# Attention with rotary embedding on one core: one q/k projection per turn with halves exchanged by DMA, and maxima turned by 128 stationary columns

## Chip, cores and metric

One Trainium2 chip, one core. The metric is the device time of one execution in microseconds (us), the median of several runs.

## The reference, cut to what matters

The whole program is a four-part network over a 2048x128 input. The change touches its first part alone, an attention layer with 16 heads of 64:

```
qkv = x @ qkv_w + qkv_b                 # x 2048x128, per head q, k, v of 2048x64
q, k = rope(q), rope(k)                 # r0 = t0*cos - t1*sin ; r1 = t1*cos + t0*sin
attn = softmax(q @ k.T / 8)             # 2048x2048 per head
out  = (attn @ v) @ out_w + out_b
x    = layernorm(x + out)
```

The other three parts (a local attention with a gated layer, a recurrent mixer, a gated layer) are left as they are.

## The kernel before, in words

`mha_heads` (from L137) computes the attention. Float32 accuracy is made of two float16 parts of each operand, so a product is three matmuls (high by high, low by high, high by low), all into float32 PSUM. The even and the odd features of a head are laid out as two halves of 32 partitions, q in partitions 0 to 63 and k in 64 to 127.

**Turns and steps.** The main loop runs over 512 steps p. A turn e is one head and one chunk of 512 queries (64 turns), and has 8 steps j; a step handles 256 keys. While turn e is attended to, the projections of turn g = e + 6 are made; they exist for the first 58 turns, e = 0 to 57. Every engine has its own list of work, written out by hand in program order, and waits only on semaphores.

**TensorE, one step (L402 to L435).** `scores(p)`: four matmuls of 512 columns into one of two PSUM buffers `p_s`. `maxima(p+12)`: two matmuls of 512 columns, one into each bank of `p_m`; each waits until VectorE has reduced what that bank held before (L341). `weigh(p-3)`: 24 matmuls of 64 or 65 columns that add up the output in `p_o`; in the turn's fourth step (j = 3) a new output begins, and its first half waits for `o_free`, that VectorE has divided and taken out the old one (L366). Beside that, in a turn: at j = 0 `project` (three matmuls of 512 columns, L302 to L304) with the weights whose halves are exchanged ("turned", L423), at j = 1 `project` with the plain ones into the same bank `p_a` once the first was read (L425, L426), at j = 5 `turn_max` (L347: the 4 columns of negated maxima are the stationary operand, a 128x128 identity moves), at j = 6 the projection of v (12 short matmuls).

**ScalarE, one step.** Two exponentials of 128x1024 (L484, L487), once in float16, once in float32. **GpSimd, one step.** One subtraction of 128x1024 (L278) that makes the low part; in one turn of four it also splits the next head's weights, 320 columns, into two parts (L239, L241).

**VectorE, in order, for a turn (L595 to L622).** Two maxima reductions per step (L542). At j = 0, between them, `rotate_sin` (L499: rot = (p_a + bias) * sin); at j = 1 `rotate_cos` (L505, in place in p_a); at j = 2, after the step's first reduction, `rotate_sum` (L511: p_a += rot), then `normalise` of the turn before (L563, L565; it posts `o_free`), then the step's second reduction. At j = 3 `negate_max` (L549) and `high` (L516), at j = 4 `low` (L522), at j = 5 `max_rows` (L555), at j = 7 the two parts of v.

**SyncE.** It issues all DMAs from one queue (L218 to L231). For each g: at a head's first chunk, the next head's weights into `w_head` (L223); after `hi_done` four copies of 64 KB from `hi` to q and k tiles (L225 to L228); after `lo_done` two more (L230, L231). None of them is needed within the turn.

Of the kernel before, what the change touches and what calls it, by code (L numbers as in the profile page):

```python
# [6 lines left out]
ALU = mybir.AluOpType  # L7
# [104 lines left out]
BY_DVE = 4  # L112
LEAD_M = 12
W_COLS = 5 * HD
W_TURNED, W_QK, W_V = slice(2 * HD, 4 * HD), slice(0, 2 * HD), slice(4 * HD, 5 * HD)

EXP_SHIFT = 12 * float(np.log(2.0)) * HD ** 0.5

# [18 lines left out]
def mha_heads(nc, x_sb, ident, a, attn, wo):  # L137

    IC = HEADS * HD // P
    with Scope(nc, "ah_") as sc:  # L140
# [12 lines left out]
        vh = sc.sb("v_hi", [P, SETS, KT, VW], F16)  # L153
        vl = sc.sb("v_lo", [P, SETS, KT, HD], F16)
        rot = sc.sb("rot_sin", [P, CH])
        hi = sc.sb("hi", [P, 2, CH], F16)
        lo = sc.sb("lo", [P, 2, CH], F16)
        part = sc.sb("part_max", [P, TPC, 4])
        negm = sc.sb("neg_max", [P, TPC], F16)
        identh = sc.sb("ident_f16", [P, P], F16)  # L160
        pb = sc.sb("probs", [P, RP, 2, CH])
        ph = sc.sb("probs_hi", [P, RW, 2, CH], F16)
# [10 lines left out]
        (ident_in, w_in, bias_in, x_turned, xh_ready, xl_ready, v_ones, zeroed, consts, w_hi_done,  # L173
         w_split, turned_ready, proj_ready, rot_done, cos_done, r_done, hi_done, lo_done, v_ready, vh_done,
         vl_done, m_ready, maxed, m_done, m_turned, mrow_ready, s_ready, exp_done, lo_pool, o_ready, rcp_done,
         o_free, wo_in, bias_turned, bias_done, biased, evac_t, evac_p) = (sc.sem(n) for n in (
             "ident_in", "w_in", "bias_in", "x_turned", "xh_ready", "xl_ready", "v_ones", "zeroed", "consts",
             "w_hi_done", "w_split", "turned_ready", "proj_ready", "rot_done", "cos_done", "r_done",
             "hi_done", "lo_done", "v_ready", "vh_done", "vl_done", "m_ready", "maxed", "m_done", "m_turned",
             "mrow_ready", "s_ready", "exp_done", "lo_pool", "o_ready", "rcp_done", "o_free", "wo_in",  # L180
             "bias_turned", "bias_done", "biased", "evac_t", "evac_p"))
        x_in = [sc.sem(f"x_in{c}") for c in range(NCH)]
        table_in = [sc.sem(f"table_in{c}") for c in range(NCH)]
        spread = [sc.sem(f"spread{b}") for b in range(2)]
        SPREAD = 6 * 16
        LAST_G = TURNS - 1

        def turned_bank(g):
# [11 lines left out]
        with nc.Block() as block:  # L200

            @block.sync
            def _(sp):
                sp.dma_start(ident[:, :], a["ident"]).then_inc(ident_in, 16)
                for c in range(NCH):
                    sp.dma_start(x_sb[:, c * TPC:(c + 1) * TPC, :],
                                 a["x"][c * CH:(c + 1) * CH, :].rearrange("(t p) d -> p t d", p=P)).then_inc(x_in[c], 16)
                    if c == 0:
                        sp.dma_start(w32[:, :], a["w_heads"][0]).then_inc(w_in, 16)
                        sp.dma_start(bqk[:, :, :], a["b_qk"]).then_inc(bias_in, 16)  # L210
                    sp.dma_start(sin[:, chunk(c)], a["sin"][:, chunk(c)]).then_inc(table_in[c], 16)
                    sp.dma_start(cos[:, chunk(c)], a["cos"][:, chunk(c)]).then_inc(table_in[c], 16)
                sp.wait_ge(w_split, 1)
                sp.dma_start(w32[:, :], a["w_heads"][1]).then_inc(w_in, 16)
                sp.dma_start(bo[:, :, :], a["b_o"]).then_inc(wo_in, 16)
                sp.dma_start(bv[:, :], a["b_v"]).then_inc(wo_in, 16)
                sp.dma_start(wo[:, :, :], a["wo_a"].rearrange("(c p) d -> p c d", p=P)).then_inc(wo_in, 16)
                for g in range(TURNS):  # L218
                    h, c = divmod(g, QC)
                    to, cs = h % SETS, chunk(c)  # L220
                    if c == 0 and 1 <= h < LAST:
                        sp.wait_ge(w_split, h + 1)
                        sp.dma_start(w32[:, :], a["w_heads"][h + 1]).then_inc(w_in, 16)  # L223
                    sp.wait_ge(hi_done, g + 1)
                    sp.dma_start(ka[0:HD, to, cs], hi[HD:P, g % 2, :]).then_inc(spread[g % 2], 16)  # L225
                    sp.dma_start(kb[HD:P, to, cs], hi[HD:P, g % 2, :]).then_inc(spread[g % 2], 16)
                    sp.dma_start(qa[0:HD, to, cs], hi[0:HD, g % 2, :]).then_inc(spread[g % 2], 16)
                    sp.dma_start(qa[HD:P, to, cs], hi[0:HD, g % 2, :]).then_inc(spread[g % 2], 16)  # L228
                    sp.wait_ge(lo_done, g + 1)
                    sp.dma_start(ka[HD:P, to, cs], lo[HD:P, g % 2, :]).then_inc(spread[g % 2], 16)  # L230
                    sp.dma_start(qb[HD:P, to, cs], lo[0:HD, g % 2, :]).then_inc(spread[g % 2], 16)  # L231

            @block.gpsimd
            def _(pool):
                def split_weights(h):
                    pool.wait_ge(w_in, 16 * (h + 1))
                    if h >= 2:
                        pool.wait_ge(v_ready, QC * (h - 1))
                    pool.tensor_copy(wh[:, h % 2, :], w32[:, :]).then_inc(w_hi_done, 1)  # L239
                    pool.wait_ge(w_hi_done, h + 1)  # L240
                    pool.tensor_tensor(wl[:, h % 2, :], w32[:, :], wh[:, h % 2, :], ALU.subtract).then_inc(w_split, 1)  # L241

                split_weights(0)
                pool.memset(vh[:, :, :, HD:VW], 1.0).then_inc(v_ones, 1)
# [39 lines left out]
            def _(pe):  # L284
# [59 lines left out]

                def turn_max(e):
                    pe.wait_ge(m_done, e + 1)
                    pe.matmul(p_a[0:TPC, 0:P], negm[:, :], identh[:, :], start=True, stop=True).then_inc(m_turned, 1)  # L347

                def scores(p):
                    e, j = divmod(p, PAIRS_A)  # L350
# [51 lines left out]
                for p in range(STEPS_A):  # L402
                    e, j = divmod(p, PAIRS_A)
                    g = e + LEAD_G
                    if j == 0:
                        pe.wait_ge(mrow_ready, e + 1)
                    last = j == LAG - 1 and p >= LAG
                    if not last:
                        scores(p)
                    if last:  # L410
                        weigh(p - LAG, 0)
                    if p + LEAD_M < STEPS_A:
                        maxima(p + LEAD_M, (0,))
                    if last:
                        weigh(p - LAG, 1)
                        scores(p)
                    elif p >= LAG:
                        weigh(p - LAG, 0)
                    if p + LEAD_M < STEPS_A:
                        maxima(p + LEAD_M, (1,))  # L420
                    if j == 0 and g <= LAST_G:
                        pe.wait_ge(vl_done, g)
                        project(turned_bank(g), g, W_TURNED, turned_ready)  # L423
                    if j == 1 and g <= LAST_G:
                        pe.wait_ge(rot_done, g + 1)  # L425
                        project(proj_bank(g), g, W_QK, proj_ready)  # L426
                    if j == 5 and e + 1 < TURNS:
                        if g <= LAST_G:
                            pe.wait_ge(lo_done, g + 1)
                        turn_max(e + 1)  # L430
                    if j == 6 and g <= LAST_G:
                        pe.wait_ge(mrow_ready, e + 2)
                        project_v(g)
                    if p >= LAG and not last:
                        weigh(p - LAG, 1)  # L435
# [55 lines left out]
            def _(dve):  # L491
                def rotate_sin(g):
# [4 lines left out]
                    if g >= 1:  # L497
                        dve.wait_ge(r_done, g)
                    dve.scalar_tensor_tensor(rot[:, :], turned_bank(g), bqk[:, 1, h:h + 1], sin[:, chunk(c)], ALU.add,  # L499
                                             ALU.mult).then_inc(rot_done, 1)  # L500

                def rotate_cos(g):
                    h, c = divmod(g, QC)
                    dve.wait_ge(proj_ready, g + 1)
                    dve.scalar_tensor_tensor(proj_bank(g), proj_bank(g), bqk[:, 0, h:h + 1], cos[:, chunk(c)], ALU.add,  # L505
                                             ALU.mult).then_inc(cos_done, 1)

                def rotate_sum(g):
                    dve.wait_ge(cos_done, g + 1)
                    dve.wait_ge(rot_done, g + 1)  # L510
                    dve.tensor_tensor(proj_bank(g), proj_bank(g), rot[:, :], ALU.add).then_inc(r_done, 1)  # L511

                def high(g):
                    dve.wait_ge(r_done, g + 1)
# [29 lines left out]

                def negate_max(e):
                    dve.wait_ge(maxed, 2 * PAIRS_A * (e + 1))
                    if e >= 1:
                        dve.wait_ge(m_turned, e)
                    dve.tensor_reduce(negm[:, :], part[:, :, :], AX, ALU.max, negate=True).then_inc(m_done, 1)  # L549

                def max_rows(e):
                    n, c = divmod(e, QC)
# [14 lines left out]

                dve.wait_ge(ident_in, 16)
                dve.tensor_copy(identh[:, :], ident[:, :]).then_inc(consts, 1)
                for c in range(NCH):  # L570
                    dve.wait_ge(xh_ready, c + 1)
                    dve.tensor_tensor(xl[:, chunk(c)], p_m[:, c % 2, :], xh[:, chunk(c)],
# [22 lines left out]
                for p in range(STEPS_A):  # L595
# [3 lines left out]
                        reduce_max(p + LEAD_M, (0,))  # L599
                    if g <= LAST_G:  # L600
                        if j == 0:
                            rotate_sin(g)
                        if j == 1:
                            rotate_cos(g)
                        if j == 2:
                            rotate_sum(g)
                        if j == 4:
                            low(g)
                    if j == LAG - 1 and e >= 1:
# [1679 lines left out]
def _layouts(i):  # L2289
# [4 lines left out]
    w = i["L0_attn_qkv_w"].reshape(D, 3, HEADS, HD)  # L2294
    order = np.concatenate([np.arange(0, HD, 2), np.arange(1, HD, 2)])
    turned = np.roll(order, HD // 2)
    a["w_heads"] = c(np.concatenate([w[:, 0][..., order], w[:, 1][..., order], w[:, 0][..., turned],
                                     w[:, 1][..., turned], w[:, 2]], -1).transpose(1, 0, 2))
    b = i["L0_attn_qkv_b"].reshape(3, HEADS, HD)
    a["b_qk"] = c(np.stack([np.concatenate([b[0][:, o], b[1][:, o]], -1).T for o in (order, turned)], 1))  # L2300
    a["b_v"] = c(b[2].reshape(HEADS * HD // P, P).T)
# [55 lines left out]
```

## Time and profile before

| what | us |
|---|---|
| median of 3 runs | 1852.96 (1850.13 to 1853.21) |
| span of the profiled execution | 1847.4 |
| one turn of the main loop, with projections | 18.20 |
| one turn of the last six, without them | about 16.8 |

The execution's own time outside its span is not given beside the profile; the median of the runs lies 5.6 us above the span. The main loop fills most of the span (some 59 us to 1216 us). It is very regular: a turn repeats with the same gaps, so a turn can be read once and multiplied. The profile names for every idle stretch of an engine what ended it; matmuls are pipelined, so the start of the next one says more of their cost than their own duration.

### The profile page before, as it was taken

To read this page: it belongs to the slowest core of one execution; us is meant where nothing else is said; L and a number is where in the kernel's file an instruction comes from. 1 tells how busy PE (TensorE), PEld (TensorE's weight loads), DVE (VectorE), ACT (ScalarE), POOL (GpSimd) and SP (SyncE) were. 2 spreads that over 40 slices of the span, in tenths; PEclk is the share of its full clock that TensorE was granted. 3 is DMA by queue.
4 is the path that set the end of the run, shared out by engine and by line. 5 is a ranking of instruction groups with operands and counts; after the bars stand their busy time and mean duration, and the time that the engine had idled before them with its cause. 6 is when DMAs were issued, how large, how long until landed. Compare 5 with 4: busy or idle time off the path is not lost. (4 is left out here: it accounts for less than half of the span.)

```text
span 1847.4 us, 53971 instructions
## 1 busy us (share of the span) xinstructions
PE 1740.1 (94%) x22856; PEld 1101.7 (60%) x22856; DVE 1444.6 (78%) x2658; ACT 1407.5 (76%) x1737; POOL 1430.4 (77%) x851
## 2 busy tenths in 40 slices
PE   5999999999999999999999999986899999978997
PEld 2466666666666666666666666675556666653454
DVE  5888888888888888888888887535988888845785
ACT  2688888888888888888888888943998888853463
POOL 6699999999999999999999999974765566624122
PEclk9899999999999999999999999998999999989998
DMA  5101010111101010101010010050111111110000
GB/s 142 25 20 31 19 31 23 27 26 28 26 24 30 21 31 19 31 23 28 23 31 23 24 26 4 2 165 18 41 40 36 37 37 37 34 26 1 1 0 24
DMA packets 71080, 56.89 MB, mean 31 GB/s; under 512 B 29196, under 2 KB 64184, under 8 KB 70840
## 3 DMA queue, kind: packets, MB, share of 16 engines
q1 hardware_dynamic: 70840, 53.44, 11.5%
q8 instruction: 181, 2.97, 0.7%
q14 instruction: 59, 0.48, 0.1%
HBM read 14.54 MB, written 1.05 MB: 8 GB/s over the span
## 5 line engine op out<-in xcount | busy, mean ns | idle before, releaser
L278 POOL TENSOR_TENSOR ah_probs_lo<-ah_probs,ah_probs_hi 128x1024 f16<-128x1024 f32 x512 | 1072.8, 2132 | 78.8 <-ACT ah_probs L487 78.7
L542 DVE TENSOR_REDUCE ah_part_max<-ah_p_m 128x1 f32<-128x512 f32 x1024 | 669.2, 685 | 120.9 <-PE ah_p_m L342 111.1
L484 ACT ACTIVATE ah_probs_hi<-ah_p_s 128x1024 f16<-128x1024 f32 x512 | 531.2, 1038 | 190.0 <-PE ah_p_s L358 178.8
L487 ACT ACTIVATE ah_probs<-ah_p_s 128x1024 f32<-128x1024 f32 x512 | 532.4, 1040 | 0.0
L372 PE MATMUL ah_p_o<-ah_v_hi,ah_probs_hi 128*128 128x65 f16 x4096 | 470.5, 195 | 5.7 <-POOL ah_probs_lo L278 5.1
L374 PE MATMUL ah_p_o<-ah_v_lo,ah_probs_hi 128*128 128x64 f16 x4096 | 470.5, 193 | 0.0
L376 PE MATMUL ah_p_o<-ah_v_hi,ah_probs_lo 128*128 128x65 f16 x4096 | 470.3, 194 | 0.0
L372 PEld LDWEIGHTS ah_p_o<-ah_v_hi,ah_probs_hi 128*128 128x128 f16 x4096 | 383.0, 98 | 84.3 <-DVE a_attn L565 12.3
L374 PEld LDWEIGHTS ah_p_o<-ah_v_lo,ah_probs_hi 128*128 128x128 f16 x4096 | 378.4, 98 | 91.3
L342 PE MATMUL ah_p_m<-ah_k_hi_lo,ah_q_hi_twice 128*128 128x512 f16 x1024 | 393.9, 385 | 6.6 <-DMA ah_max_q_lo<-ah_lo 3.1
L357 PE MATMUL ah_p_s<-ah_q_hi_twice,ah_k_hi_lo 128*128 128x512 f16 x1024 | 388.6, 379 | 0.8 <-ACT ah_probs L487 0.4
L358 PE MATMUL ah_p_s<-ah_max_q_lo,ah_one_k_hi 128*128 128x512 f16 x1024 | 388.4, 379 | 0.0
L376 PEld LDWEIGHTS ah_p_o<-ah_v_hi,ah_probs_lo 128*128 128x128 f16 x4096 | 379.2, 98 | 0.0
L342 PEld LDWEIGHTS ah_p_m<-ah_k_hi_lo,ah_q_hi_twice 128*128 128x128 f16 x1024 | 100.2, 98 | 82.2 <-DVE ah_part_max L542 15.1
L357 PEld LDWEIGHTS ah_p_s<-ah_q_hi_twice,ah_k_hi_lo 128*128 128x128 f16 x1024 | 100.2, 98 | 70.3 <-ACT ah_probs L487 1.4
L358 PEld LDWEIGHTS ah_p_s<-ah_max_q_lo,ah_one_k_hi 128*128 128x128 f16 x1024 | 100.1, 98 | 68.6 <-issue 0.4
L1032 POOL TENSOR_TENSOR ba_rot_sum<-ba_rot_parts 128x512 f32<-128x512 f32 x64 | 80.1, 1274 | 60.0 <-DVE ba_rot_parts L1417 60.0
L1055 POOL TENSOR_TENSOR ba_qk<-ba_rot_sum,ba_rnorm 128x1024 f32<-128x1024 f32 x32 | 60.9, 1903 | 73.5 <-issue 72.8
L1417 DVE TENSOR_TENSOR ba_rot_parts<-ba_p_qk,bw_rot 128x1024 f32<-128x1024 f32 x64 | 75.4, 1218 | 31.9 <-ACT ba_sq L1318 31.4
L1047 POOL TENSOR_TENSOR ba_probs_lo<-ba_probs,ba_probs_hi 128x1024 f16<-128x1024 f32 x32 | 68.2, 2130 | 6.1 <-ACT ba_probs L1327 6.1
L505 DVE SCALAR_TENSOR_TENSOR ah_p_a<-ah_p_a,ah_bias_qk,ah_cos 128x512 f32<-128x512 f32 x58 | 44.0, 759 | 30.8 <-PE ah_p_a L304 30.8
L499 DVE SCALAR_TENSOR_TENSOR ah_rot_sin<-ah_p_a,ah_bias_qk,ah_sin 128x512 f32<-128x512 f32 x58 | 43.6, 751 | 31.4 <-PE ah_p_a L304 31.4
(316 smaller groups left out, 3090.0 us busy)
## 6 DMA issues: line engine op xcount, KB each, us to landing
ba_v_skew<-ba_v_own SPq DMA_DIRECT2D x64, 129.0 KB, 2.3
ah_q_hi_twice<-ah_hi SPq DMA_DIRECT2D x128, 64.0 KB, 2.0
ah_k_hi_lo<-ah_hi SPq DMA_DIRECT2D x64, 64.0 KB, 1.9
ah_one_k_hi<-ah_hi SPq DMA_DIRECT2D x64, 64.0 KB, 2.0
ah_k_hi_lo<-ah_lo SPq DMA_DIRECT2D x64, 64.0 KB, 2.0
ah_max_q_lo<-ah_lo SPq DMA_DIRECT2D x64, 64.0 KB, 2.0
ah_w_head<-in_w_heads SPq DMA_DIRECT2D x16, 160.0 KB, 2.4
bw_rot<-in_rot SPq DMA_DIRECT2D x4, 512.0 KB, 10.3
```

Source lines behind the costliest of these rows:

```text
L278: pool.tensor_tensor(pl[:, p % RW, :, :], pb[:, p % RP, :, :], ph[:, p % RW, :, :], ALU.subtract).then_inc(lo_pool, 1)
L342: pe.matmul(p_m[:, b, :], qa[:, s, rows], ka[:, s, chunk(2 * half + b)], start=True, stop=True).then_inc(m_ready, 1)
L357: pe.matmul(p_s[:, p % 2, i, :], ka[:, s, ks], qa[:, s, chunk(c)], start=True, stop=False)
L358: mm = pe.matmul(p_s[:, p % 2, i, :], kb[:, s, ks], qb[:, s, chunk(c)], start=False, stop=True)
L372: pe.matmul(o, hi_i, vh[:, s, kt, :], start=(kt == 0 and i == 0), stop=False, skip_group_check=True)
L374: pe.matmul(o[:, 0:HD], hi_i, vl[:, s, kt, :], start=False, stop=False, skip_group_check=True)
L376: mm = pe.matmul(o, lo_i, vh[:, s, kt, :], start=False, stop=(kt == KT - 1), skip_group_check=True)
L484: act.activation(ph[:, p % RW, :, :], p_s[:, p % 2, :, :], ACT.Exp, scale=HD ** -0.5)
L487: act.activation(pb[:, p % RP, :, :], p_s[:, p % 2, :, :], ACT.Exp, scale=HD ** -0.5).then_inc(exp_done, 1)
L542: dve.tensor_reduce(part[:, t, 2 * half + b:2 * half + b + 1], p_m[:, b, :], AX, ALU.max).then_inc(maxed, 1)
L1032: pool.tensor_tensor(out[:, :, :, f, :], part[:, :, 0, :, f, :], part[:, :, 1, :, 1 - f, :], ALU.add).then_inc(t3_done, 1)
L1417: dve.tensor_tensor(t12[:, s, :, :].rearrange("p r (h d) -> p r h d", d=DH), x4.unsqueeze(1).to_broadcast([P, 2, HEADS_B, DH]), lw.tab[:, ...
```

## The change

Only one projection of q and k per turn is made in the main loop (j = 0), with the plain weights. VectorE multiplies it by the sine into a new tile `half` (at j = 0, posting `sin_done`), and by the cosine in place (j = 1). SyncE waits for `sin_done` and copies the four blocks of 32 partitions of `half` into `rot`, exchanged in pairs (0 and 1, 2 and 3), with four DMAs of 64 KB. At j = 2 VectorE waits for all four (`swapped`) and subtracts `rot`. The six turns ahead of the loop are as before. The weights' columns are put in another order, so that heads from the third on load and split 192 columns and not 320. The maxima tile has 128 columns, 124 of them zero, so that `turn_max` has 128 stationary columns and writes 128 rows, of which 4 are used.

```
-W_TURNED, W_QK, W_V = slice(2 * HD, 4 * HD), slice(0, 2 * HD), slice(4 * HD, 5 * HD)
+W_QK, W_V, W_TURNED = slice(0, 2 * HD), slice(2 * HD, 3 * HD), slice(3 * HD, 5 * HD)
+W_LATER = 3 * HD
...
+        half = sc.sb("sin_part", [P, CH])
...
-        negm = sc.sb("neg_max", [P, TPC], F16)
+        negm = sc.sb("neg_max", [P, P], F16)
...
+        SWAP = 4 * 16
+        HALF_A = HD // 2
...
                     if c == 0 and 1 <= h < LAST:
                         sp.wait_ge(w_split, h + 1)
-                        sp.dma_start(w32[:, :], a["w_heads"][h + 1]).then_inc(w_in, 16)
+                        sp.dma_start(w32[:, 0:W_LATER], a["w_heads"][h + 1][:, 0:W_LATER]).then_inc(w_in, 16)
+                    if g >= LEAD_G:
+                        sp.wait_ge(sin_done, g - LEAD_G + 1)
+                        sp.wait_ge(r_done, g)
+                        for b in range(4):
+                            sp.dma_start(rot[(b ^ 1) * HALF_A:((b ^ 1) + 1) * HALF_A, :],
+                                         half[b * HALF_A:(b + 1) * HALF_A, :]).then_inc(swapped, 16)
                     sp.wait_ge(hi_done, g + 1)
...
-                    pool.tensor_copy(wh[:, h % 2, :], w32[:, :]).then_inc(w_hi_done, 1)
+                    cols = slice(0, W_COLS if h * QC < LEAD_G else W_LATER)
+                    pool.tensor_copy(wh[:, h % 2, cols], w32[:, cols]).then_inc(w_hi_done, 1)
                     pool.wait_ge(w_hi_done, h + 1)
-                    pool.tensor_tensor(wl[:, h % 2, :], w32[:, :], wh[:, h % 2, :], ALU.subtract).then_inc(w_split, 1)
+                    pool.tensor_tensor(wl[:, h % 2, cols], w32[:, cols], wh[:, h % 2, cols],
+                                       ALU.subtract).then_inc(w_split, 1)
...
-                    pe.matmul(p_a[0:TPC, 0:P], negm[:, :], identh[:, :], start=True, stop=True).then_inc(m_turned, 1)
+                    pe.matmul(p_a[:, 0:P], negm[:, :], identh[:, :], start=True, stop=True).then_inc(m_turned, 1)
...
                     if j == 0 and g <= LAST_G:
                         pe.wait_ge(vl_done, g)
-                        project(turned_bank(g), g, W_TURNED, turned_ready)
-                    if j == 1 and g <= LAST_G:
-                        pe.wait_ge(rot_done, g + 1)
                         project(proj_bank(g), g, W_QK, proj_ready)
...
+                def times_sin(g):
+                    h, c = divmod(g, QC)
+                    dve.wait_ge(proj_ready, g + 1)
+                    if g > LEAD_G:
+                        dve.wait_ge(swapped, SWAP * (g - LEAD_G))
+                    dve.scalar_tensor_tensor(half[:, :], proj_bank(g), bqk[:, 0, h:h + 1], sin[:, chunk(c)], ALU.add,
+                                             ALU.mult).then_inc(sin_done, 1)
...
+                def minus_swapped(g):
+                    dve.wait_ge(cos_done, g + 1)
+                    dve.wait_ge(swapped, SWAP * (g - LEAD_G + 1))
+                    dve.tensor_tensor(proj_bank(g), proj_bank(g), rot[:, :], ALU.subtract).then_inc(r_done, 1)
...
+                    if e == 0:
+                        dve.wait_ge(negm_zeroed, 1)
...
-                    dve.tensor_reduce(negm[:, :], part[:, :, :], AX, ALU.max, negate=True).then_inc(m_done, 1)
+                    dve.tensor_reduce(negm[:, 0:TPC], part[:, :, :], AX, ALU.max, negate=True).then_inc(m_done, 1)
...
+                dve.memset(negm[:, :], 0.0).then_inc(negm_zeroed, 1)
...
                         if j == 0:
-                            rotate_sin(g)
+                            times_sin(g)
                         if j == 1:
+                            dve.wait_ge(sin_done, g - LEAD_G + 1)
                             rotate_cos(g)
                         if j == 2:
-                            rotate_sum(g)
+                            minus_swapped(g)
```

## Rows read from the trace of the kernel before

**Rows 1.** The page: busy time of the engines, share of the span, instructions.

```profile
PE 1740.1 (94%) x22856; PEld 1101.7 (60%) x22856; DVE 1444.6 (78%) x2658; ACT 1407.5 (76%) x1737; POOL 1430.4 (77%) x851
```

**Rows 2.** Stretch, then busy PE, PEld, DVE, ACT, POOL, granted clock, DMA; a late turn.

```profile
629.60:647.80 18.20, 18.20 (x262) 11.54 (x261) 15.39 (x28) 15.19 (x18) 16.75 (x8) 1.00 0.09 23
1132.60:1149.40 16.80, 16.68 (x248) 10.70 (x247) 11.81 (x21) 15.29 (x17) 16.80 (x9) 1.00 0.01 2
```

**Rows 3.** Timeline of TensorE in one turn: start, duration, instruction, output<-inputs.

```profile
622.08 0.38 PE L302 MATMUL ah_p_a<-ah_xT_hi,ah_w_hi 128*128 128x512 f16 x1
...
622.72 0.19 PE L372 MATMUL ah_p_o<-ah_v_hi,ah_probs_hi 128*128 128x65 f16 x1
...
623.08 0.38 PE L357 MATMUL ah_p_s<-ah_q_hi_twice,ah_k_hi_lo 128*128 128x512 f16 x1
...
633.38 0.38 PE L342 MATMUL ah_p_m<-ah_k_hi_lo,ah_q_hi_twice 128*128 128x512 f16 x1
633.69 0.22 PE L347 MATMUL ah_p_a<-ah_ident_f,ah_neg_max 128*4 128x128 f16 x1
633.84 0.20 PE L372 MATMUL ah_p_o<-ah_v_hi,ah_probs_hi 128*128 128x65 f16 x1
```

**Rows 4.** Timeline of VectorE in the same turn.

```profile
622.92 0.75 DVE L499 SCALAR_TENSOR_TENSOR ah_rot_sin<-ah_p_a,ah_bias_qk,ah_sin 128x512 f32<-128x512 f32 x1 [0.54 <-PE ah_p_a L304]
...
625.59 0.76 DVE L505 SCALAR_TENSOR_TENSOR ah_p_a<-ah_p_a,ah_bias_qk,ah_cos 128x512 f32<-128x512 f32 x1 [0.53 <-PE ah_p_a L304]
...
627.45 0.69 DVE L511 TENSOR_TENSOR ah_p_a<-ah_p_a,ah_rot_sin 128x512 f32<-128x512 f32 x1
628.25 0.42 DVE L565 TENSOR_TENSOR a_attn<-ah_p_o,ah_rcp 128x256 f32<-128x256 f32 x1
628.60 1.88 DVE L542 TENSOR_REDUCE ah_part_max<-ah_p_m 128x1 f32<-128x512 f32 x3
...
630.59 0.68 DVE L516 CAST ah_hi<-ah_p_a 128x512 f16<-128x512 f32 x1
...
641.12 0.75 DVE L499 SCALAR_TENSOR_TENSOR ah_rot_sin<-ah_p_a,ah_bias_qk,ah_sin 128x512 f32<-128x512 f32 x1 [0.54 <-PE ah_p_a L304]
```

**Rows 5.** The two maxima matmuls of TensorE in the step j = 3.

```profile
628.63 0.38 PE L342 MATMUL ah_p_m<-ah_k_hi_lo,ah_q_hi_twice 128*128 128x512 f16 x1
...
629.33 0.39 PE L342 MATMUL ah_p_m<-ah_k_hi_lo,ah_q_hi_twice 128*128 128x512 f16 x1
```

**Rows 6.** Timeline of SyncE's DMA issues in one turn.

```profile
631.30 0.46 SPq L225 DMA_DIRECT2D ah_k_hi_lo<-ah_hi  x1
...
633.09 0.60 SPq L228 DMA_DIRECT2D ah_q_hi_twice<-ah_hi  x1
```

**Rows 7.** DMA issues: count, KB each, median us from the issue's start to landing.

```profile
ah_q_hi_twice<-ah_hi SPq DMA_DIRECT2D x128, 64.0 KB, 2.0
...
ba_v_skew<-ba_v_own SPq DMA_DIRECT2D x64, 129.0 KB, 2.3
ah_w_head<-in_w_heads SPq DMA_DIRECT2D x16, 160.0 KB, 2.4
...
g_ident<-in_ident SPq DMA_DIRECT2D x1, 64.0 KB, 1.8
```

**Rows 8.** Issues at the start: two loads, and the last copy before the first maxima.

```profile
2.67 0.43 SPq L211 DMA_DIRECT2D ah_sin<-in_sin  x1
3.14 0.43 SPq L212 DMA_DIRECT2D ah_cos<-in_cos  x1
...
35.12 0.60 SPq L231 DMA_DIRECT2D ah_max_q_lo<-ah_lo  x1
```

**Rows 9.** TensorE's wait for that copy.

```profile
37.28 0.59 PE L342 MATMUL ah_p_m<-ah_k_hi_lo,ah_q_hi_twice 128*128 128x512 f16 x2 [3.09 <-DMA ah_max_q_lo<-ah_lo]
```

**Rows 10.** Groups of 100 to 1200 us: GpSimd's splitting of weights.

```profile
L241 POOL TENSOR_TENSOR ah_w_lo<-ah_w_head,ah_w_hi 128x320 f16<-128x320 f32 x13 | 10.3, 791 | 1.0
L239 POOL CAST ah_w_hi<-ah_w_head 128x320 f16<-128x320 f32 x13 | 5.8, 450 | 0.0
```

More of the change, by code:

```diff
@@ L175, in mha_heads @@
          vl_done, m_ready, maxed, m_done, m_turned, mrow_ready, s_ready, exp_done, lo_pool, o_ready, rcp_done,
-         o_free, wo_in, bias_turned, bias_done, biased, evac_t, evac_p) = (sc.sem(n) for n in (
+         o_free, wo_in, bias_turned, bias_done, biased, evac_t, evac_p, sin_done, swapped,
+         negm_zeroed) = (sc.sem(n) for n in (
              "ident_in", "w_in", "bias_in", "x_turned", "xh_ready", "xl_ready", "v_ones", "zeroed", "consts",
@@ L180, in mha_heads @@
              "mrow_ready", "s_ready", "exp_done", "lo_pool", "o_ready", "rcp_done", "o_free", "wo_in",
-             "bias_turned", "bias_done", "biased", "evac_t", "evac_p"))
+             "bias_turned", "bias_done", "biased", "evac_t", "evac_p", "sin_done", "swapped",
+             "negm_zeroed"))
         x_in = [sc.sem(f"x_in{c}") for c in range(NCH)]
@@ L2296, in _layouts @@
     turned = np.roll(order, HD // 2)
-    a["w_heads"] = c(np.concatenate([w[:, 0][..., order], w[:, 1][..., order], w[:, 0][..., turned],
-                                     w[:, 1][..., turned], w[:, 2]], -1).transpose(1, 0, 2))
+    a["w_heads"] = c(np.concatenate([w[:, 0][..., order], w[:, 1][..., order], w[:, 2],
+                                     w[:, 0][..., turned], w[:, 1][..., turned]], -1).transpose(1, 0, 2))
     b = i["L0_attn_qkv_b"].reshape(3, HEADS, HD)
```

## The prediction, made before the changed kernel was run

> **What bounds the kernel now.** I read the page's busy times first [rows 1]: TensorE is busy for 94% of the span, the other engines for under 80%. Busy time of pipelined matmuls proves little, so I read one turn in stretches [rows 2]: of 18.20 us TensorE shows no gap, VectorE works 15.39, ScalarE 15.19 and GpSimd 16.75. The last six turns have no projections, and there GpSimd has no gap: a turn takes 16.80 us, and that is the floor that the next engine sets. So TensorE binds the 58 turns with projections, and up to 1.4 us a turn could be gained before GpSimd binds.
>
> Then I looked for the small waits inside TensorE's turn, because that is where a delayed VectorE would enter. In step j = 3 it issues the first maxima matmul at 628.63, twelve short matmuls behind it, and the second maxima matmul at 629.33 [rows 5]. Twelve short ones take 0.36 us elsewhere in the turn (622.72 to 623.08 [rows 3]), and the matmul ahead of them 0.22, so this one could have gone at about 629.21. What it waited for is on VectorE [rows 4]: rotate_sum starts at 627.45, then come the reciprocal, the multiply that frees the output at 628.25, and the reduction that frees this maxima bank, at 628.60; it is the first of three in 1.88 us, and ends at about 629.28. So the second maxima matmul of j = 3 goes 1.88 us after rotate_sum starts. TensorE waits about 0.12 us there already: **VectorE has no slack at j = 2 and 3**, and the change puts its new wait exactly in front of rotate_sum's place.
>
> **The change part by part.**
>
> *One projection less.* Three matmuls of 512 columns go: the first starts at 622.08 and the next work at 622.72 [rows 3], so 0.64 us a turn leave TensorE.
>
> *turn_max with 128 stationary columns.* Now the maxima matmul before it starts at 633.38, it at 633.69, the next short matmul at 633.84 [rows 3]. A matmul of 512 columns occupies 0.215 us (three in 0.64), so 0.46 - 0.215 = 0.245 us belong to turn_max, for 128 moving columns that are worth 0.054 at the same pace. Beside full 128-column loads, short matmuls follow each other in 0.03 us (twelve in 0.36), so a full load hides well; I take 0.05 for the new form and a gain of 0.19. The bounds are 0 and 0.19. In the Trainium skill, "TensorE: Matmul & The Clock Gate", section "LDWEIGHTS (loading the stationary operand)", the load time grows with the columns (columns / 1.2 in ns), which speaks against this part: 4 columns would be 3 ns and 128 columns 107 ns, a loss of 0.10 us a turn as an estimate; its section on weight-path modes says that the fast load needs just 128 columns, which speaks for it. The rows of the short matmuls side with the second.
>
> *The new wait.* times_sin takes the place of rotate_sin at j = 0, with the same start and 0.75 us. rotate_cos no longer waits 0.53 us for a second projection [rows 4], so VectorE would reach the subtraction early, at about 627.45 - 0.53 = 626.92, 4.0 us after times_sin began. The exchanged halves come later than that. SyncE picks a posted result up in 0.03 us: `high` ends at 630.59 + 0.68 = 631.27 [rows 4] and the issue starts at 631.30 [rows 6]. Of four issues on end the fourth starts 1.79 us after the first, about 0.6 apart [rows 6]. A 64 KB copy within SBUF lands 2.0 us after its issue began [rows 7]. One arrival can be seen directly: issued at 35.12 [rows 8], TensorE goes on at 37.28 [rows 9], which is 2.16 with the pick-up by a TensorE just out of idleness. I take 2.0 + 0.05. From the end of times_sin to the start of the subtraction that is 0.03 + 1.79 + 2.05 = 3.87 us, from its start 0.75 + 3.87 = 4.62 us, against 4.0 without the wait and 4.53 (622.92 to 627.45) before. VectorE stands idle 0.6 us, with normalise and the reduction queued behind it, and TensorE waits for both.
>
> *The cycle.* From the second maxima matmul of j = 3 (629.33) to the next turn's rotate_sin (641.12) TensorE sets the pace: 11.79 us; nothing of the removed projection lies in it, turn_max does: 11.60 after. Then 4.62 to the subtraction, then 1.88 as before. Turn after: 11.60 + 4.62 + 1.88 = **18.10 us**, against 11.79 + 4.53 + 1.88 = 18.20. Check from TensorE's side: 18.20 - 0.64 - 0.19 - 0.12 (the old wait) = 17.25 of work; so it waits 0.85 us in each turn, where it waited 0.12. Nearly all that the projection saves is given back in that wait.
>
> *The bounds of the exchange.* Landing: 1.8 (a 64 KB load) to 2.3 (129 KB within SBUF) or 2.4 (160 KB) [rows 7]; the new copies have 32 rows of 2 KB and not 64 of 1 KB, nearest to the spread copies in bytes and place, so 2.0. Issues: from 0.47 apart (two loads at the start [rows 8]), which brings the last start to 1.4, to 0.6 apart. With both low the chain would be 0.6 us shorter, which VectorE's own 4.0 us just cover. The turn could be 17.5 to 18.5 (landing 2.4). In the Trainium skill, "DMA: Bandwidth & Descriptors", section "Anatomy of one DMA — SWDGE (gpsimd) path", a copy costs about 2.0 us plus bytes/436e3, 2.15 us for 64 KB as an estimate; with it the turn is 18.20 and the gain is gone. It is fitted for another issuing engine; the rows have 2.0.
>
> *Costs taken as nothing.* GpSimd splits 192 columns for 320: 1.24 us [rows 10] become about 0.75, one turn in four; GpSimd has 1.4 us of gap a turn, so neither counts, and a turn of 17.5 would still be above GpSimd's 16.75 + 0.19. SyncE issues four more DMAs (2.4 us) and is idle most of the turn; hi's copies come after the subtraction, so nothing of theirs is late. The weights' load comes ahead of the exchange on the same queue every fourth turn, but its own wait ended in the turn before. The memset at the start lies in VectorE's wait for x. In the six last turns GpSimd binds and turn_max gains nothing.
>
> **Sum.** 58 x (18.20 - 18.10) = 5.8 us: a span of 1841.6, and a median of 1852.96 - 5.8 = about **1847 us** (the median lies 5.6 above the span, which I leave so).
>
> **The rivals.**
>
> 1. *The swap is slower than the spread copies* (landing 2.2 to 2.4, or VectorE picks up later). From 0.10 us more on the chain, nothing is gained; each further 0.1 us costs 5.8 us. At 2.3, as the 129 KB copies [rows 7]: a turn of 18.40, 58 x 0.20 = 12 us more, 1865. For it: rows twice as long, in quarters of the partitions; the one direct arrival shows 2.16 [rows 8, 9]. Against: the bytes are those of the spread copies. It ends slower. The skill's fit above would put the case at its lower edge, with no change.
> 2. *The exchange is partly hidden*: issues 0.47 apart and the same landing give 18.10 - 0.39 = 17.71, a gain of 58 x 0.49 = 28 us, 1825. For it: the loads at the start [rows 8]; against: the copies from SBUF in the loop are 0.6 apart [rows 6].
> 3. *It is wholly hidden*: then VectorE's own work sets the subtraction, 4.0 us after times_sin starts, and the turn is 11.60 + 4.0 + 1.88 = 17.48, a gain of 42 us, 1811. With issues as in the rows it needs a landing of 1.4 us, which no row shows.
> 4. *turn_max gains nothing* with the forecast chain, its full load standing in the open as the 4-column one does: a turn of 18.29, 58 x 0.09 = 5 us slower, 1858. Against it: the pace of the short matmuls. By the skill's rule for loads, a further 0.10 us would go, 18.39 and 1864.
>
> **Chances.** The forecast with its near side (17.9 to 18.14): 0.40; rival 2: 0.12; rival 3: 0.03; so faster by over 0.2% 0.55. Within 0.2% (3.7 us, what a measurement of this kernel can tell from no change; turns of 18.14 to 18.26): 0.17. Rival 1 beyond that 0.22, rival 4 0.06: slower 0.28. Range: from a turn of 17.75 (1827) to one of 18.4 (1865); what is left out is the far end of rival 2, rival 3 and a landing above 2.3. The likeliest case's own range is 1836 to 1850.
>
> **What the profile would show.** Right: a turn of about 18.1 us; a wait of VectorE ended by the DMA into the rotated tile, about 0.6 us, 58 times; no wait of L505's for TensorE; the subtraction 4.6 us after times_sin starts; TensorE idle about 0.8 us at j = 3, released by VectorE's multiply or reduction; short matmuls 0.05 us after turn_max. Wrong: no DMA wait on VectorE; TensorE's wait at another place (maxima of j = 5, the low parts of GpSimd); issues of the exchange not 0.6 apart; a granted clock below the 1.00 of these turns [rows 2].

## The result and the profile after

The changed kernel takes 1879.24 us (median of 4), the kernel before 1851.55 beside it: ratio 1.0153, 95% interval 1.0136 to 1.017, some 28 us **slower**, outside the range that was given (1827 to 1865). The profiled execution took 1878.78 us with a span of 1876.7.

The main waits of the changed kernel from 100 to 1200 us (who waited for whom: us in total, times, longest):

```profile
PEld ah_p_o L386 <- DVE a_attn L591: 84.4, 56, 2.4
DVE ah_p_a L535 <- DMA ah_rot_sin<-ah_sin_part: 65.0, 55, 2.1
PE ah_p_o L386 <- DVE a_attn L591: 56.9, 56, 1.9
DVE ah_sin_part L518 <- PE ah_p_a L318: 29.4, 55, 0.5
PEld ah_p_m L356 <- DVE ah_part_max L566: 10.1, 56, 0.2
```

The wait is where it was forecast: VectorE at the subtraction (L535) waits for the copies, and TensorE at j = 3 waits for VectorE's multiply (L591). But the mean is 65.0 / 55 = 1.18 us and the longest 2.1, where 0.6 was forecast for each. So I read two turns. First turn 14 (counting from 0), VectorE, the counterpart of [rows 4]:

```profile
313.06 0.75 DVE L518 SCALAR_TENSOR_TENSOR ah_sin_part<-ah_p_a,ah_bias_qk,ah_sin 128x512 f32<-128x512 f32 x1 [0.53 <-PE ah_p_a L318]
...
317.79 0.70 DVE L535 TENSOR_TENSOR ah_p_a<-ah_p_a,ah_rot_sin 128x512 f32<-128x512 f32 x1 [0.74 <-DMA ah_rot_sin<-ah_sin_part]
318.40 0.17 DVE L589 RECIPROCAL ah_rcp<-ah_p_o 128x4 f32<-128x4 f32 x1
318.61 0.42 DVE L591 TENSOR_TENSOR a_attn<-ah_p_o,ah_rcp 128x256 f32<-128x256 f32 x1
...
331.28 0.75 DVE L518 SCALAR_TENSOR_TENSOR ah_sin_part<-ah_p_a,ah_bias_qk,ah_sin 128x512 f32<-128x512 f32 x1 [0.53 <-PE ah_p_a L318]
```

The turn is 331.28 - 313.06 = 18.22 us (the shortest are 18.20), the subtraction starts 4.73 us after the sine product (4.62 forecast), and from there to the next sine product 13.49 us pass (11.60 + 1.88 = 13.48 forecast). TensorE, the same turn, the counterpart of [rows 5] and of the end of [rows 3]:

```profile
319.69 0.39 PE L356 MATMUL ah_p_m<-ah_k_hi_lo,ah_q_hi_twice 128*128 128x512 f16 x1
...
323.96 0.22 PE L361 MATMUL ah_p_a<-ah_ident_f,ah_neg_max 128*128 128x128 f16 x1
324.02 0.19 PE L386 MATMUL ah_p_o<-ah_v_hi,ah_probs_hi 128*128 128x65 f16 x1
```

The second maxima matmul of j = 3 goes at 319.69, 1.90 us after the subtraction starts; behind turn_max the next matmul follows in 0.06 us. Now turn 20, VectorE, then SyncE's four issues in it:

```profile
424.72 0.75 DVE L518 SCALAR_TENSOR_TENSOR ah_sin_part<-ah_p_a,ah_bias_qk,ah_sin 128x512 f32<-128x512 f32 x1 [0.53 <-PE ah_p_a L318]
...
430.74 0.70 DVE L535 TENSOR_TENSOR ah_p_a<-ah_p_a,ah_rot_sin 128x512 f32<-128x512 f32 x1 [2.03 <-DMA ah_rot_sin<-ah_sin_part]
```

```profile
425.50 2.45 SPq L234 DMA_DIRECT2D ah_rot_sin<-ah_sin_part  x4
```

The issues take the same 2.45 us as in turn 14 (313.84 to 316.29), yet the subtraction starts 6.02 us after the sine product: the copies land 1.3 us late. The source of L234 gives that for all 232 copies:

```profile
DMA to landing us min/median/max: 1.9/2.0/3.3
```

**What delays them** is in the DMA queues of short stretches. From 313 to 317.8 (the copies of turn 14) there is no line but the first queue's; from 424.8 to 430.7 (turn 20) there are two (packets, MB, share of 16 engines):

```profile
q1 hardware_dynamic: 192, 0.26, 18.4%
q8 instruction: 1, 0.02, 1.5%
```

One instruction fetch is one packet of 16 KB, and 1.5% of 16 engines over 5.9 us is 1.4 us on one of them. The DMA records of turn 20 show what it holds up. A copy is 32 packets of 2 KB and 16 of 4 bytes; in turn 14 all 192 packets of the four copies have begun 4.32 us after the sine product. In turn 20, 186 have. The other six (four of 2 KB and two of 4 bytes, a sixteenth of two copies) run one after another from 4.53 to 5.40, and the fetch, begun at 3.17, ends at 4.54: one engine's share of the last two copies stood behind it. Listed from the same records (when in the turn the fetches of 16 KB begin, counted from the sine product; landing matters from about 0.8, the first issue, to 4.7):

```
turn          turn us   sine to subtraction   fetches begin at
2 to 16       18.2        4.7                 5.0 to 8.3,  13.6 to 15.0
17            19.32       5.84                3.28, 14.63
20            21.15       6.02                3.17, 16.48
27            19.18       5.69                2.73, 13.18
33            19.30       5.81                2.52, 12.92
41            19.19       5.70                0.93, 12.66
46            18.21       4.73                0.15, 12.29
51            18.21       4.73                9.57
```

Of the 30 turns over 18.3 us 28 have such a fetch that begins between 0.6 and 3.8; no turn of 18.2 us has one between 0.6 and 4.7. The other two met a smaller fetch of 8 KB, from a second instruction queue (q14): turn 13, in the first line but 18.48 us long, at 3.0, and turn 47 (18.61) at 3.6. The small ones matter less: turns 1, 9, 11 and 49 met one at 2.3 to 2.6 and took 18.2 us. In some turns the fetch also holds up an issue; in turn 30 the four issues take 3.64 us and not 2.45:

```profile
620.48 3.64 SPq L234 DMA_DIRECT2D ah_rot_sin<-ah_sin_part  x4
```

Fetches come twice a turn and drift slowly through it, so they meet the copies in some half of the turns. In three turns (20, 21, 30) TensorE's wait of about 1.8 us was followed by a stretch at the lower clock, its matmuls of 512 columns taking 0.62 us in the rows for 0.38. Turns 19, 24 and 31, with a wait of 1.8 us too, had none, and what decides it is open. Busy times of the turns 14, 28 and 30 (the last numbers are granted clock, DMA share, GB/s):

```profile
313.06:331.28 18.22, 17.57 (x262) 11.16 (x259) 15.39 (x27) 15.40 (x17) 17.31 (x9) 1.00 0.16 38
582.05:600.89 18.84, 17.56 (x262) 11.14 (x259) 15.39 (x27) 15.40 (x17) 16.88 (x9) 1.00 0.15 37
619.70:640.72 21.02, 19.19 (x262) 12.00 (x259) 15.40 (x27) 15.40 (x17) 17.10 (x9) 0.92 0.14 33
```

The books: summed over the turns, the subtraction starts 24 us later than at 4.73 us in each. Of these, 20 us lie between the last issue and the subtraction, and 4 us ahead of the last issue, which starts up to 1.0 us late in ten turns (13, 38 to 45, 47). The three turns with a stretch at 1.2 GHz have 1.6 us more behind it each, 5 us. That is 29 us, against 29.3 us by which the two spans differ. Undisturbed turns win and lose nothing.

### The profile page after: what moved, and what is told of

Read it like the earlier page. It is cut to its first block and busy times, and to the rows that moved or that the text cites. A ratio compares the mean times of both kernels' runs of the same rounds, so it can differ in the third digit from the quotient of the medians.

```text
span 1876.7 us, 53958 instructions
## 1 busy us (share of the span) xinstructions
PE 1706.5 (91%) x22682; PEld 1084.0 (58%) x22682; DVE 1445.8 (77%) x2659; ACT 1419.1 (76%) x1737; POOL 1430.7 (76%) x851
## 5 line engine op out<-in xcount | busy, mean ns | idle before, releaser
L498 ACT ACTIVATE ah_probs<-ah_p_s 128x1024 f32<-128x1024 f32 x512 | 525.4, 1026 | 0.0
L535 DVE TENSOR_TENSOR ah_p_a<-ah_p_a,ah_rot_sin 128x512 f32<-128x512 f32 x58 | 40.6, 700 | 67.4 <-DMA ah_rot_sin<-ah_sin_part 67.4
L518 DVE SCALAR_TENSOR_TENSOR ah_sin_part<-ah_p_a,ah_bias_qk,ah_sin 128x512 f32<-128x512 f32 x58 | 43.6, 751 | 31.1 <-PE ah_p_a L318 31.1
```

The costliest lines, as they stand in the source:

```text
L498: act.activation(pb[:, p % RP, :, :], p_s[:, p % 2, :, :], ACT.Exp, scale=HD ** -0.5).then_inc(exp_done, 1)
```

## The experiments

All ratios are to the kernel before, run beside each.

**e1_turn4**: turn_max alone undone.

```
-        negm = sc.sb("neg_max", [P, P], F16)
+        negm = sc.sb("neg_max", [P, TPC], F16)
-                    pe.matmul(p_a[:, 0:P], negm[:, :], identh[:, :], ...)
+                    pe.matmul(p_a[0:TPC, 0:P], negm[:, :], identh[:, :], ...)
```

> The changed kernel with turn_max back at 4 stationary columns. Theory (the turn is the chain from the sine product over the four copies to the subtraction, then 1.9 us to TensorE's second maxima matmul of j = 3, then TensorE's own pace, in which turn_max lies): an undisturbed turn goes from 18.21 to 18.40 us, some 11 us more in all, about 1.021 of the kernel before. Rival (turn_max is not on the path, or the wide load costs as much): 18.21 stays, ratio as the changed kernel, 1.015.

1894.41 us, 1.0246 (1.021 to 1.0281). The undisturbed turn is 18.41 us, as the theory has it; TensorE's time between the chain's ends is on the path, and the wide load wins 0.20 us a turn. By the two ratios the total is 17 us above the changed kernel's, for the 11 us expected; its trace has four turns with a stretch at the lower clock, not three.

**e2_before_turn128**: turn_max alone done, in the kernel before (the wide, zeroed tile and `p_a[:, 0:P]`, as in the change).

> The kernel before with turn_max at 128 stationary columns alone. Theory: a turn goes from 18.20 to 18.01 us, 11 us less, about 0.994. Rival: the wide load stands in the open, 0 to 0.1 us a turn more, 1.000 to 1.003.

1835.79 us, 0.9932 (0.9904 to 0.9959); turns of 18.00 us. This half of the change alone gains 12 us.

**e3_no_wait**: the four copies stay, nobody waits for them; the subtraction takes the sine product with its halves not exchanged.

```
                     dve.wait_ge(cos_done, g + 1)
-                    dve.wait_ge(swapped, SWAP * (g - LEAD_G + 1))
-                    dve.tensor_tensor(proj_bank(g), proj_bank(g), rot[:, :], ALU.subtract)...
+                    dve.tensor_tensor(proj_bank(g), proj_bank(g), half[:, :], ALU.subtract)...
```

> The changed kernel, all four copies issued as before, but the subtraction reads the sine product itself and waits for no copy (the rotation is left wrong). Theory (only the wait for the landing costs, not the traffic): no turn is longer than the others, the subtraction starts 4.0 us after the sine product, a turn of 17.4 to 17.5 us, 42 to 46 us below the kernel before, about 0.976. Rival (the copies' traffic or the removed projection's order slows other work): turns of 18.8 us and more remain in the middle of the loop, ratio 1.00 or above.

1802.86 us, 0.9753 (0.9725 to 0.9781). Every turn takes 17.37 to 17.54 us, the middle ones too. The copies' traffic costs nothing that shows, and the whole distance to the changed kernel (1.0153 - 0.9753, 74 us) is the wait for landing.

**e9_two_copies**: `for b in range(4)` becomes `range(2)`, `SWAP` 2 * 16; blocks 2 and 3 are not copied.

> The changed kernel with two of the four copies left out (half of the rotated tile is stale). Theory: the last issue starts 1.3 us earlier, so in an undisturbed turn VectorE's own 4.0 us decide, a turn of 17.4 to 17.5 us; where a fetch meets a copy up to 18.1; about 0.98 of the kernel before. Rival (the landing of all bytes or the wait itself costs, not the row of issues): 18.0 us and more in undisturbed turns.

1811.62 us, 0.9798 (0.9778 to 0.9819). Undisturbed turns take 17.38 us, as in e3: without the last two issues (1.18 us in SyncE's timeline, not 2.45) VectorE's own work decides, as expected. Turns 28 to 37 still take 18.06 to 18.53, more than the 18.1 expected: a shorter chain meets fewer fetches, but pays for each. Its waits, 100 to 1150 us, with only 13 left:

```profile
DVE ah_p_a L535 <- DMA ah_rot_sin<-ah_sin_part: 8.4, 13, 1.1
```

**e10_full_split**: load and split of all 320 columns again.

```
-                        sp.dma_start(w32[:, 0:W_LATER], a["w_heads"][h + 1][:, 0:W_LATER])...
+                        sp.dma_start(w32[:, :], a["w_heads"][h + 1])...
-                    cols = slice(0, W_COLS if h * QC < LEAD_G else W_LATER)
+                    cols = slice(0, W_COLS)
```

> The changed kernel with the narrower load and split of weights undone (320 columns for every head). Theory: GpSimd has idle time in every turn, nothing changes: 1.013 to 1.020 of the kernel before, as the changed kernel. Rival (GpSimd binds in the turns with a split): 2 to 8 us more.

1876.58 us, 1.0151 (1.0133 to 1.017), as the changed kernel: this part costs and wins nothing here.

**e6_phase**: is it the fetches, and whose? 64 tiny matmuls ahead of the loop, 128 instructions on TensorE.

```
+                for _ in range(64):
+                    pe.matmul(p_a[:, 0:1], identh[:, :], xh[:, 0:1], start=True, stop=True)
                 pe.wait_ge(wo_in, 3 * 16)
```

> The changed kernel with 64 matmuls of one column added on TensorE ahead of the loop (128 instructions more, results unused). Theory (TensorE's instruction fetches, 16 KB in one packet of about 1.2 us on one DMA engine, twice a turn, delay a copy that they meet between its issue and its landing; they drift slowly through the turn because a turn has some instructions over 512): the fetches come half a period earlier, so the long turns are no longer turns 17 to 47 but those up to about 18 and those from about 45 on, and turns 20 to 40 take 18.2 us. Rival (the long turns belong to a place in the loop, to the clock or to a head's data): turns 17 to 47 stay long.

1860.08 us, 1.0061 (1.004 to 1.0082), 17 us less than the changed kernel by the two ratios, for added work. The long turns have moved:

```
turn          turn us            fetches begin at
1 to 3        19.01 to 19.17     1.1 to 2.5, 12.4 to 12.8
7             18.48              0.92, 11.75
12            18.20              11.48
23            18.21              8.83, 16.71
35            18.21              7.95, 15.51
54            19.11              3.38, 14.50
56            18.97              3.22, 14.34
```

From turn 10 to 53 nearly all take 18.2 us, where most were long before; four (13, 26, 41, 47) take 18.37 to 18.56, and each met a fetch of 8 KB. The long turns are fewer than was expected: 1 to 8, 54 and 56, not all up to 18 and from 45 on. The same wait from 300 to 900 us, of the changed kernel and then of this one:

```profile
DVE ah_p_a L535 <- DMA ah_rot_sin<-ah_sin_part: 47.2, 32, 2.1
```

```profile
DVE ah_p_a L537 <- DMA ah_rot_sin<-ah_sin_part: 25.4, 33, 1.1
```

1.48 us a turn became 0.77, with the same code in the loop. The rival, a place in the loop, falls; the fetches are TensorE's, since instructions on TensorE alone moved them.

**e5_sub_late**, **e8_sub_mid**, **e4_sub_after**: the subtraction at three later places of VectorE's order. e5 has it right before `high` at j = 3, e8 at j = 3 behind the first reduction (`if j == 2` becomes `if j == 3`), e4 at j = 2 behind normalise and the second reduction:

```
                         if j == 1:
                             dve.wait_ge(sin_done, g - LEAD_G + 1)
                             rotate_cos(g)
-                        if j == 2:
-                            minus_swapped(g)
...
+                    if j == 2 and g <= LAST_G:
+                        minus_swapped(g)
                     if j == 3 and e + 1 < TURNS:
                         negate_max(e + 1)
```

> The changed kernel with the subtraction moved on VectorE from j = 2 (ahead of normalise) to j = 3, right before high. Theory: the copies have 2 us more to land, so even a landing that is 1.3 us late is hidden; no wait for the copies is left, a turn of 17.3 to 17.5 us all along, about 0.976 of the kernel before. Rival (the chain of p_a's users, low before turn_max, takes over as the bound): 17.8 to 18.2 us.

1821.3 us, 0.9853 (0.9822 to 0.9884). No wait for a copy is left, but all turns take 17.70 us, between theory and rival. What took over is VectorE's dense stretch, TensorE's maxima waiting for its reductions (100 to 1150 us):

```profile
DVE ah_part_max L566 <- PE ah_p_m L356: 110.4, 203, 1.1
...
PEld ah_p_m L356 <- DVE ah_part_max L566: 34.3, 112, 0.4
```

The timeline of that kernel shows where VectorE was idle instead, ahead of this stretch:

```profile
310.04 0.68 DVE L566 TENSOR_REDUCE ah_part_max<-ah_p_m 128x1 f32<-128x512 f32 x1
311.07 1.29 DVE L566 TENSOR_REDUCE ah_part_max<-ah_p_m 128x1 f32<-128x512 f32 x2 [0.35 <-PE ah_p_m L356]
312.39 0.17 DVE L575 TENSOR_REDUCE ah_neg_max<-ah_part_max 128x4 f16<-128x16 f32 x1
312.48 0.69 DVE L535 TENSOR_TENSOR ah_p_a<-ah_p_a,ah_rot_sin 128x512 f32<-128x512 f32 x1
```

> The changed kernel with the subtraction at j = 3 of VectorE, behind that step's first reduction (high stays behind the step's second one). Theory: VectorE has an idle stretch of 0.35 us there in the version with the subtraction right before high, and its dense stretch up to turn_max is what made that turn 17.70; a turn of 17.3 to 17.5 us where no fetch meets the copies, at most 17.8 where one does, 0.975 to 0.985 of the kernel before. Rival (the subtraction's place does not matter for the dense stretch, or the exposed landing costs more than it wins): 0.985 or above.

1811.39 us, 0.9798 (0.9783 to 0.9813). Turns of 17.57 us, slightly over what was expected of the undisturbed ones; the longest of the disturbed ones is 17.90.

> The changed kernel with the subtraction at j = 2 of VectorE, behind normalise and the step's second reduction (one reduction earlier than in the version at j = 3 that ran 17.57 us a turn). Theory: VectorE sits idle 0.36 us just behind that place, so the subtraction half fills a gap, and the copies have landed by then unless a fetch meets them: 17.37 to 17.45 us in undisturbed turns, up to 18.0 in the disturbed ones, 0.975 to 0.981 of the kernel before. Rival (the reduction queued behind the wait is needed at once by TensorE): undisturbed turns of 17.6 or more, disturbed ones above 18.2, 0.983 or more.

**1805.39 us, 0.9767 (0.9749 to 0.9786)**: 43 us below the kernel before and 71 us below the change as it was made (by the ratios), by the place of one instruction. Undisturbed turns take 17.22 us, less than expected, and every fourth of them 17.60. Turns 2 and 3 (busy times of TensorE, its loads, VectorE, ScalarE, GpSimd):

```profile
91.53:109.13 17.60, 17.39 (x262) 11.23 (x259) 15.34 (x28) 15.09 (x17) 17.60 (x10) 1.00 0.16 39
109.13:126.35 17.22, 17.22 (x262) 11.18 (x259) 15.20 (x28) 15.09 (x17) 16.80 (x9) 1.00 0.17 40
```

In the 17.22 us turn TensorE has no gap, and GpSimd one of 0.4 us: TensorE's own work binds it, for which the forecast's check had 17.25. In the 17.60 us turn GpSimd has no gap. It split the next head's weights in the turn before (0.35 and 0.55 us), and TensorE then waits for its low part:

```profile
94.07 0.20 PE L386 MATMUL ah_p_o<-ah_v_hi,ah_probs_hi 128*128 128x65 f16 x1 [0.21 <-POOL ah_probs_lo L292]
```

This wait stands at the same place in each of the eight undisturbed turns of 17.60 us, and in none of 17.22. It is 0.2 of the 0.38 us; that the split causes the rest too is read from the trace, and no run tests it. Turns that meet a fetch still take up to 18.28 us.

## Why the prediction was wrong

*The bound and the cycle* were right. From the subtraction over the second maxima matmul of j = 3 to the next sine product it forecast 13.48 us, and nearly every turn has 13.48 or 13.49; e1 and e2 move it by the 0.20 us of turn_max (0.19 forecast), e3 opens it to 17.38 (17.48 forecast for rival 3; VectorE reaches the subtraction 3.90 us after the sine product starts, not 4.0).

*turn_max*: the upper bound, 0.19, is what came (0.20). In the Trainium skill, "TensorE: Matmul & The Clock Gate", the rule on fast loads (128 columns, section on weight-path modes) agrees with e2's 0.20 us; the one in its section on LDWEIGHTS, by which the wide load would cost 0.10 us, does not. Rival 4 falls.

*The exchange in an undisturbed turn* was undersized by 0.11 us: the last issue starts 1.86 us after the first (2.45 less its own 0.59; 1.79 forecast), and the subtraction follows it in 2.09 (2.05 forecast). That alone takes the forecast gain of 0.10 us a turn away: 18.21 against 18.20. The fit in the Trainium skill's "DMA: Bandwidth & Descriptors" (section on the anatomy of one DMA), 2.15 us, gave that same turn, but not for its reason: the median landing is 2.0, and the row of issues made up most of the rest.

*The step that failed* is "A 64 KB copy within SBUF lands 2.0 us after its issue began [rows 7] ... I take 2.0 + 0.05", a median taken for every turn. It is the right median (2.0 again) and the wrong number for a chain without slack: the landing has a tail to 3.3 us, in ten turns the last issue itself starts late, and so in half of the turns the subtraction is late, and each delay is paid in full. It was worth 24 us, with the clock 29. Rival 1 had the direction and the price (5.8 us per 0.1 us) but looked for the reason in the copies' shape; a chain 0.4 us longer in the mean is what came. The tail could be seen in the trace of before: SyncE's timeline has 21 issues of 0.8 to 2.1 us among those of 0.6 in the main loop, the queue of fetches has 181 packets, and the copies of L231, 64 KB like the new ones, have this:

```profile
DMA to landing us min/median/max: 2.0/2.0/3.5
```

Nothing waited for the copies there, so it cost nothing.

*The costs taken as nothing* were nothing (e10, and the traffic by e3), except one: the forecast named a fall of the clock only as a sign of error. GpSimd's split begins to count only in the shorter turns of e4. *The rivals 2 and 3* fall as descriptions of this kernel; e4 gets below rival 3's turn (17.22 against 17.48), through VectorE's order and not through quicker copies.

## What to carry to other kernels

When a transfer comes onto the path of every iteration, take its whole distribution and not its median, and look in the trace of before for what shares the DMA engines, instruction fetches among them: what was harmless behind slack is paid in full without it. Before a producer is moved to a DMA, look for the latest place at which its consumer can wait without anything queued behind it being due; here one instruction's place was worth 4% of the kernel. A waiting instruction's neighbours matter as much as its own slack: e5, with most slack for the copies, was slower than e4.

## What was not expected of the hardware

TensorE's instruction fetches travel on the same DMA engines as the kernel's copies, 16 KB in one packet of 0.9 to 1.6 us (DMA records), and a 64 KB copy that meets one lands up to 1.3 us later. An issue on SyncE that meets one takes up to 1.8 us, not 0.6. The place of the fetches in the loop drifts, and 128 unneeded instructions ahead of the loop changed the time by 1%.
